# A layer norm centred by one matmul, its weights and biases folded away, and projections in 64-row tiles

## The reference, cut to what matters

```
def layernorm(x, w, b):                      # over the 64 channels of a position
    mu = mean(x); var = mean(square(x - mu))
    return (x - mu) * rsqrt(var + EPS) * w + b
x_ln = layernorm(x, ln1_w, ln1_b)
q, k, v = split(einsum('bhwc,oc->bohw', x_ln, qkv_w))          # 4 heads of 16
attn = softmax(q k / sqrt(16)); out = attn v                   # full attention, 1024 x 1024 per head
x = x + proj_w out + proj_b
x_ln2 = layernorm(x, ln2_w, ln2_b)
x = x + fc2_w gelu(fc1_w x_ln2 + fc1_b) + fc2_b                # fc1: 64 -> 128
t = t + window_attention(norm(t)) + bu       # 8 heads, 32 keys a query; norm without weights
t = t + recurrence(norm(t))                  # W x, batch norm, 1024 steps of sigmoid(wx + V y)
```

## Time and profile before

| | before |
|---|---|
| runs | 498.24, 501.23, 499.96: median 499.96 us |
| profiled execution | 499.44 us, its span 497.6 us |
| TensorE busy | 445.2 us (89%), granted clock 0.977 on the mean |
| VectorE busy | 327.3 us (66%), of that 166.6 in the 256 row maxima |
| ScalarE busy | 289.9 us (58%) |
| GpSimd busy | 12.9 us, all at the start |
| chain that ended last | 63% TensorE, 24% VectorE, 7% ScalarE, 3% DMA |

### The profile page before, as it was taken

The page is one execution under the profiler, slowest core; times in us unless marked ns, Lnnn a source line. Parts: engine busy times, 40 slices in busy tenths (PEclk is TensorE's granted clock), DMA queues, the critical chain, the costliest instruction groups (busy, mean ns, idle before and its releaser), DMA issues.

```text
span 497.6 us, 7934 instructions
## 1 busy us (share of the span) xinstructions
PE 445.2 (89%) x3257; PEld 176.3 (35%) x3257; DVE 327.3 (66%) x605; ACT 289.9 (58%) x499; POOL 12.9 (3%) x15
## 2 busy tenths in 40 slices
PE   7786999979999998899999996999999889986883
PEld 2323322223234332232243432232433323542583
DVE  2599887999778566598688474798522654524414
ACT  4342677747774673566955771678586656083342
POOL 9000000000000000000000000000000000000000
PEclk9898999999999999899999998999999999999997
DMA  7200180004500000017100000000000000000003
GB/s 293 57 1 2 29 162 3 0 2 100 91 2 1 1 1 1 1 29 147 16 2 1 1 1 2 1 1 0 3 1 1 1 0 2 1 1 1 1 1 86
DMA packets 6196, 13.09 MB, mean 26 GB/s; under 512 B 1296, under 2 KB 3600, under 8 KB 6032
## 3 DMA queue, kind: packets, MB, share of 16 engines
q1 hardware_dynamic: 6160, 12.58, 11.3%
HBM read 9.07 MB, written 3.41 MB: 25 GB/s over the span
## 4 chain that ended last, share of the span: by engine, by line
PE 63%; DVE 24%; ACT 7%; DMA 3%; issue 2%; SPq 1%; DVEq 0%; ACTq 0%
DVE part_max L1181 10%; PE O L750 9%; PE R L798 6%; PE T L735 5%; PE T L715 4%; PE R L907 3%; PE R L654 3%; PE R L735 3%; PE R L646 3%; PE R L868 2%; PE R L715 2%; PE R L882 2%; PE T L626 2%; PE R L895 2%; DMA KX<-qk_scratch 2%
## 5 line engine op out<-in xcount | busy, mean ns | idle before, releaser
L1181 DVE TENSOR_REDUCE part_max<-T 128x1 f32<-128x512 f32 x166 | 107.0, 681 | 25.3 <-PE T L715 25.2
L1041 ACT ACTIVATE probs<-T 128x512 f32<-128x512 f32 x149 | 83.8, 600 | 26.8 <-PE T L735 26.4
L1041 ACT ACTIVATE probs<-R 128x512 f32<-128x512 f32 x107 | 60.7, 601 | 31.2 <-PE R L735 31.0
L750 PE MATMUL O<-probs,VT 128*32 128x512 f32 x512 | 68.3, 606 | 0.0
L1181 DVE TENSOR_REDUCE part_max<-R 128x1 f32<-128x512 f32 x90 | 59.6, 682 | 3.9 <-PE R L715 3.9
L715 PE MATMUL T<-KX,QX 96*128 96x512 bf16 x166 | 56.2, 387 | 4.1 <-DVE part_max L1181 2.1
L735 PE MATMUL T<-QX,KX 99*128 99x512 bf16 x149 | 51.4, 386 | 3.9 <-DVE part_max L1181 1.8
L735 PE MATMUL R<-QX,KX 99*128 99x512 bf16 x107 | 37.2, 382 | 0.5 <-ACT VT L1026 0.3
L715 PE MATMUL R<-KX,QX 96*128 96x512 bf16 x90 | 31.3, 384 | 0.6 <-DVE part_max L1181 0.3
L715 PEld LDWEIGHTS T<-KX,QX 96*128 96x128 bf16 x166 | 15.1, 98 | 43.2 <-DVE part_max L1181 15.7
L798 PE MATMUL R<-xp,abd 128*128 128x512 f32 x64 | 30.0, 600 | 0.2 <-DVE xp L1150 0.2
(11 more groups left out here) (220 smaller groups left out, 636.1 us busy)
## 6 DMA issues: line engine op xcount, KB each, us to landing
qk_scratch<-qk_part SPq DMA_DIRECT2D x6, 384.0 KB, 4.5
zs<-early SPq DMA_DIRECT2D x1, 2048.0 KB, 9.2
QX<-qk_scratch SPq DMA_DIRECT2D x3, 384.0 KB, 5.3
KX<-qk_scratch SPq DMA_DIRECT2D x3, 384.0 KB, 7.0
result<-probs SPq DMA_DIRECT2D x2, 512.0 KB, 5.1
s_rest<-rest SPq DMA_DIRECT2D x1, 882.0 KB, 13.1
X<-x SPq DMA_DIRECT2D x2, 384.0 KB, 13.0
QX<-qk_scratch SPq DMA_DIRECT2D x3, 256.0 KB, 7.8
```

The source lines that it names most:

```text
L750: last = mm(O[h * HP:(h + 1) * HP, :], VT[b % 2][:, j, h, :], probs[:, u % 2, h, :], start=(j == 0), stop=(j == KT - 1))
L1041: A(probs[:, u % 2, h, :], ring["scores", b, u, h], ACT.Exp, scale=HD ** -0.5).then_inc(g["exp_done"], 1)
L1181: nc.vector.tensor_reduce(part_max[:, row, kh:kh + 1], ring["max_piece", b, half, i], AX_X, ALU.max).then_inc(g["max_red"], 1)
```

## The change

A norm has one VectorE instruction where it had two or three. `center`, the unit matrix less `mean_c`, takes the place of `mean_c` in the first product, so PSUM holds the centred rows at once; ScalarE squares them from PSUM, and VectorE makes the normalised rows from PSUM and the reciprocal root. The norm's weight goes into that instruction as its scalar. The norm's bias goes behind the products: `wq`, `wk` and `wfc1` are multiplied by the bias once, and the result is the bias of the ScalarE copy (`qk_bias`), of the Gelu (`fc1_bias`), and, for V, through the output projection, of `proj_bias`. These need four one-column products in the first projection and three in `products`.

Q, K and fc1 are made in 64-row tiles. PSUM bank R0 now holds the positions of half 0, Q in its lower 64 partitions and K in its upper 64, and bank R1 those of half 1, the other way round. So the three parts are written to DRAM by four transfers an image instead of two, and, as `RUNS` pairs the parts anew, read back by eight instead of six. The places of all four tables are new.

```
-RUNS = (((0, 2), (1, 1), (2, 0)), ((0, 1), (1, 0)), ((0, 0),))
+RUNS = (((0, 0), (1, 1)), ((0, 1), (0, 2)), ((1, 0), (2, 0)))
-FIRST = {"mean_c": P, "vectors": len(VECTORS), "eye": C, "wq": P, "wk": P, "wv": P}
+FIRST = {"mean_c": P, "center": P, "vectors": len(VECTORS), "eye": C, "wq": P, "wk": P, "wv": P}
 MAX_AT = (                          # one line of each table is shown
-        118, 118, 118, 119, 119, 119, 121, 121, 121, 123, 126, 127, 127, 132, 134, 134, 135, 135, 135, 139, 139, 139,
+        112, 112, 116, 117, 117, 117, 118, 118, 118, 119, 122, 122, 125, 127, 129, 130, 132, 137, 137, 137, 137, 139,
 LAYER_AT = (
-    0, 0, 3, 5, 15, 16, 21, 320, 316, 318, 328, 334, 343, 346, 348, 353, 353, 371, 384, 402, 411, 413, 421, 424,
+    0, 1, 1, 4, 9, 14, 14, 320, 320, 321, 323, 326, 337, 342, 350, 352, 353, 370, 370, 406, 408, 411, 411, 413,
...
+        def qk_rows(q, half):
+            return half_rows(q ^ half)
...
             def relayout(b):
                 for half in range(2):
-                    sp.dma_start(scratch[b, half].rearrange("q r d h n -> (d h) (q r) n"),
-                                 qk_rows[half_rows(half), :, :]).then_inc(g["qk_dram"], 16)
+                    for q in range(2):
+                        sp.dma_start(scratch[b, half, q].rearrange("r d h n -> (d h) r n"),
+                                     qk_part[qk_rows(q, half), half, :, :]).then_inc(g["qk_dram"], 16)
...
                     for q, dst in enumerate((QX[b % 2], KX[b % 2])):
+                        parts = sorted({term[q] for term in run_})
+                        p0, n = parts[0], len(parts)
+                        for again in range(len(run_) // n):
+                            at = row + again * HD
+                            sp.dma_start(dst[at:at + n * HD, :, :, :].rearrange("p a h n -> p a (h n)"), ...
...
             def ln_mean(b, which, i):        # TensorE
-                mm(ln_bank(b, which, i, 0), t["mean_c"], ln_in(b, which, i), start=True, stop=True).then_inc(g["ln_mean"], 1)
+                mm(ln_bank(b, which, i, 0), t["center"], ln_in(b, which, i), start=True, stop=True).then_inc(g["ln_ctr"], 1)
             def project(b):                  # TensorE
+                    for half in range(2):    # first image only
+                        for q, w in enumerate(("wq", "wk")):
+                            last = mm(bias_bank(half)[qk_rows(q, half), 0:1], t[w][half_rows(half), half_rows(half)], v["ln1_b"][half_rows(half), :],
+                                      start=True, stop=True)
+                        last.then_inc(g["bias_mm"], 1)
-                mm(R[:, 0, :], t["wq"], x_ln[:], start=True, stop=True).then_inc(g["qk_mm"], 1)
-                mm(R[:, 1, :], t["wk"], x_ln[:], start=True, stop=True).then_inc(g["qk_mm"], 1)
+                for half in range(2):
+                    for q, w in enumerate(("wq", "wk")):
+                        last = mm(R[qk_rows(q, half), half, :], t[w][half_rows(half), half_rows(half)], x_ln[half_rows(half), :],
+                                  start=True, stop=True)
+                    last.then_inc(g["qk_mm"], 1)
             def fc1(b):                      # TensorE
-                    last = mm(pair(b)[:, half, :], t["wfc1"][:, half, :], x_ln[:], start=True, stop=True)
+                    last = mm(pair(b)[:, half, :], t["wfc1"][half_rows(half), half, :], x_ln[half_rows(half), :], start=True, stop=True)
             def products():                  # TensorE
+                mm(R[:, 1, 0:1], t["wv"], v["ln1_b"], start=True, stop=True)
+                mm(R[:, 1, 1:2], t["wfc1"][0:C, 0, :], v["ln2_b"][0:C, :], start=True, stop=True).then_inc(g["fold_mm"], 1)
...
+                pe.wait_ge(g["fold_done"], 2)
+                mm(R[:, 1, 2:3], t["wproj_c"], v_bias[:], start=True, stop=True).then_inc(g["fold_mm"], 1)
             def ln_square(b, which, i):      # ScalarE
-                A(ln_bufs(b, which, i)["ln_q"], ln_bufs(b, which, i)["ln_d"], ACT.Square).then_inc(g["ln_sq"], 1)
+                A(ln_bufs(b, which, i)["ln_q"], ln_bank(b, which, i, 0), ACT.Square).then_inc(g["ln_sq"], 1)
             def project(b):                  # ScalarE
-                    A(hi_rows[:, q, :], R[:, q, :], ACT.Copy).then_inc(g["qk_hi"], 1)
+                    A(hi_rows[:, half, :], R[:, half, :], ACT.Identity, bias=qk_bias[:, half:half + 1]).then_inc(g["qk_hi"], 1)
-            def ln_mean(b, which, i):        # VectorE
-                TT(ln_bufs(b, which, i)["ln_d"], ln_in(b, which, i), ln_bank(b, which, i, 0), ALU.subtract).then_inc(g["ln_ctr"], 1)
             def ln_scale(b, which, i):       # VectorE
-                TT(ln_dst(b, which, i), buf["ln_d"], buf["ln_r"], ALU.mult).then_inc(g["ln_norm"], 1)
                 if which < 3:
-                    dve.wait_ge(g["ln_norm"], ln_no(b, which, i) + 1)
-                    TS(x_ln[:], ln_dst(b, which), v[f"ln{which}_w"], v[f"ln{which}_b"], ALU.mult, ALU.add).then_inc(g["ln_out"], 1)
+                    last = STT(dst, centered, v[f"ln{which}_w"], buf["ln_r"], ALU.mult, ALU.mult)
+                else:
+                    last = TT(dst, centered, buf["ln_r"], ALU.mult)
+                last.then_inc(g["ln_norm"], 1)
             def project(b):                  # VectorE
-                    TT(qk_rest[:, q, :], R[:, q, :], hi_rows[:, q, :], ALU.subtract).then_inc(g["qk_rst"], 1)
+                    STT(qk_rest[:, half, :], R[:, half, :], qk_bias[:, half:half + 1], hi_rows[:, half, :], ALU.add, ALU.subtract).then_inc(g["qk_rst"], 1)
...
+    arr["center"] = np.eye(P, dtype=f) - arr["mean_c"]
```

More of the change, by code:

```diff
@@ L435, in ln_dst @@
         def ln_dst(b, which, i=0):
+            if which < 3:
+                return x_ln[:, :]
             if which == 3:
                 return xn
-            return ln_bufs(b, which, i)["ln_d"] if which < 3 or (b, which) == (B - 2, 4) else xh[:, ln_cols(b, which, i)]
+            return ln_bufs(b, which, i)["ln_d"] if (b, which) == (B - 2, 4) else xh[:, ln_cols(b, which, i)]
         def pair(b):
@@ L447, in build @@
         LAID = 4 * H0 - 1
+        QK_READS = sum(len(r) // len({term[q] for term in r}) for r in RUNS for q in range(2))
         def laid(h, n):
@@ L692, in relay @@
                         for half in range(2):
-                            rows = sel[half_rows(half), q, r, :, h:C:H0].rearrange("p t d -> p (t d)")
-                            last = mm(lay_bank(q, half)[0:KQ, :], rows, qk_rows[half_rows(half), PARTS * q + r, :],
+                            rows = sel[qk_rows(q, half), q, k, :, h:C:H0].rearrange("p t d -> p (t d)")
+                            last = mm(lay_bank(q, half)[0:KQ, :], rows, qk_part[qk_rows(q, half), half, k, :],
                                       start=(k == 0), stop=(k == PARTS - 1))
@@ L1013, in project @@
                 elif b:
[L1014 to L1017 removed]
+                    act.wait_ge(g["qk_dram"], 64 * (b - 1))
+                else:
+                    act.wait_ge(g["bias_done"], 2)
+                for half in range(2):
+                    act.wait_ge(g["qk_mm"], 2 * b + half + 1)
+                    A(hi_rows[:, half, :], R[:, half, :], ACT.Identity, bias=qk_bias[:, half:half + 1]).then_inc(g["qk_hi"], 1)
             def project_v(b):
@@ L1320, in _ @@
             dve.wait_ge(g["first_in"], 16)
-            run({"masks": masks, "relay": relay, "ln_mean": ln_mean, "ln_scale": ln_scale, "project": project, "split": split,
+            run({"masks": masks, "relay": relay, "ln_scale": ln_scale, "project": project, "split": split,
                  "o_norm": o_norm_, "round": round_keys, "wx": wx_part, "max_piece": max_piece, "max_neg": max_neg,
@@ L1448 @@
     arr["wproj"] = wp
+    arr["wproj_c"] = both(g["L0_conv_proj_w"].T)
     w1 = np.zeros((P, 2, P), f)
```

109 lines of the change are left out of this document (59 added, 50 removed), and 18 rows, old and new, of the table LAYER_AT.

## The result

The changed kernel took 484.38 us (median of 4 runs, 480.5 to 488.32) against 500.6 of before: the ratio is 0.9645, 95% interval 0.9579 to 0.9711. Run twice more beside the experiments it stood at 0.9718 (0.9647 to 0.9789) and 0.9701 (0.9651 to 0.975). The forecast was 489.5, a ratio of 0.978: the sign was right, the gain was too small. The ratios and intervals leave out executions over 1.5% above the fastest of their kernel, here the one of 488.32 us, which is also the profiled one (span 486.5, TensorE's mean granted clock 0.973), so the end in its trace is worse than in most.

The account below looks back on a forecast made before the run. VectorE bounds 25 to 125 us, TensorE 125 to 390, chains through the engines both ends; -3.1 + 0.9 - 0.75 - 1.0 - 4.2 - 2.2 = -10.35 from 499.44 gives 489.1, plus 0.5 for the median, rounded: 489.5 us; range 483.5 to 495.5.

Parts of the forecast that it names:

- Part 1: First norm and projection, 0 to 22 us: one merged normalising instruction and tiled projection bring the low parts earlier, -3.1 us.
- rival E: First norm: the memset holds the normalising instruction, 2.4 us less gain, 491.9 us; counted within the forecast's 0.58.
- B: Tiles don't overlap as the nearest rows do: 0.85 us back at six places, 494.6 us; 0.19 shared by three rivals.
- Part 2: At 37 us: three products for the folded biases stand unhidden on TensorE around the weight products, +0.9 us.
- Part 3: Second image's norm, projection and transfers, 44 to 77 us: 1.03 + 0.6 gained, 0.9 given back to writes, -0.75 us.
- rival D: Transfers cost by their number: +5.2 - 0.9 us at 77 us, 493.8 us; 0.19 shared by three rivals.
- Part 4: Third image, 77 to 125 us: the same removal on VectorE, transfers stay hidden, -1.0 us.
- Part 5: TensorE's stretch, 125 to 390 us: -3.4 for fc1 and projection tiles, 0.8 of idle time back, -4.2 us.
- Rival A: 125 to 390 us: lighter VectorE shrinks TensorE's idle by 4 to 8 us, 482 to 486 us; chance 0.13.
- Rival C: ScalarE's exponentials or the new order hold TensorE, 125 to 390 us gains nothing, 493.7 us; 0.19 shared by three rivals.
- Rival G: New places stop TensorE's in-order queue between 125 and 390 us: slower, 503 at 10% idle, 509 at 12%; chance 0.06.
- Part 6: The end, 390 to 470 us: fc1 tiles -0.9, third norm -0.7, fourth norm -0.6, together -2.2 us.

Follow-up runs that it names:

- e7: Changed kernel plus an idle VectorE subtraction, result never used, at the 17 places where the real one stood: 0.9691 of before, 484.78 us.
- e8: Kernel before with GpSimd's memset of KX put behind the first image's x_ln: 502.44 us, one execution.

## Why the forecast was off

Part 1 (-3.1): right, -3.29. The normalising instruction took 0.75 beside the memset, so rival E fell, and the projection's 8 records took 1.09 at a clock of 1.00, so B fell. What the prediction did not see is that the clock fell behind it, at 20 us, and took back 1.3 in the profiled execution.

Part 2 (+0.9): right, +0.89 for the length of these products; between the row maxima on either side of them it is 0.7. Three products stood alone on TensorE.

Part 3 (-0.75): -1.9 was measured (from -1.28 at the first image's first transposed maxima, 43.30 in before, to -3.22 at the second image's first row maximum), and the term that failed is the +0.9 for the writes. Answering to the earlier trace rows, the four writes and the row maxima that wait for the reads:

```profile
55.71 2.63 SPq L570 DMA_DIRECT2D qk_scratch<-qk_part  x4
...
60.81 0.34 SPq L582 DMA_DIRECT2D QX<-qk_scratch  x1
...
72.99 0.60 PE L737 MATMUL R<-KX,QX 96*128 96x512 bf16 x2
```

```profile
73.41 1.29 DVE L1216 TENSOR_REDUCE part_max<-R 128x1 f32<-128x512 f32 x2 [2.96 <-PE R L737]
```

The same two of before, the first read and the first product that needs the reads:

```profile
64.51 0.34 SPq L568 DMA_DIRECT2D QX<-qk_scratch  x1
...
76.20 0.61 PE L715 MATMUL T<-KX,QX 96*128 96x512 bf16 x2 [0.30 <-DMA KX<-qk_scratch]
```

The first read was issued 5.10 us after the first write, where with two writes of twice the size it was 5.45: nothing given back. The eight reads took 0.5 more than the six (12.18 and 11.69 us from the first one's issue to the first product that needs them), so writes and reads together cost 0.14, not 0.9. The split itself came 2.1 earlier, where 1.6 was forecast. VectorE was dry for 2.96 us (3.33 before), so rival D fell. That the sum of the first three parts is right within 0.3 (-3.22 against -2.95) is luck: this error and the clock's 1.3 cancel.

Part 4 (-1.0): right, -1.14 to the end of the projection back.

Part 5 (-4.2): the step that failed; 10.5 was measured. Both of its terms were wrong. "-3.4" for the tiles: fc1's share of it, 2.6, was worth 0.3, as ScalarE's queue decides fc2; the projection's share was not measured. "I let 0.8 come back" took VectorE's and the norms' relief as something that could at most shrink 14.3 us of idle time; the runs show that a norm between TensorE's products holds TensorE wherever too little work stands between its two products, and that in the new places 10.4 us hung on the nine subtractions: 6.4 of idle time and 4.0 of busy time, mostly at the low clock that followed the first wait. So the premise that "the latency of a norm counts in full only at both ends" failed. The prediction priced a shorter norm against the idle time of the old order, 14.3 us, of which only 1.9 stood ahead of variances, and not against what the new order would idle without it. By busy and idle time the gain even looks as forecast for the tiles (TensorE 6.43 less busy: 3.4 of tiles, some 2.7 of clock), which is bookkeeping, not cause: take fc1's tiles away and only 0.3 goes. Nor did the "some 247 us of work" of the prediction's signs follow from its own sum, 246.78 less 3.4 for the tiles; 240.35 was measured.

Rival A had the size (idle down by 4 to 8 us, 482 to 486 in all) and the wrong cause: VectorE's load, which by e7 costs nothing in the middle. Rival C described correctly what happens to fc1, and missed the rest. Rival G, the new places as a loss, is true of the places alone: 1% slower with the old arithmetic. The prediction took the places for neutral, because most had moved by less than five of 320 (38 of the 241 places of `MAX_AT` differ by five to eleven); they were what turned a shorter norm into time.

Part 6 (-2.2): right while the clock was up, -2.24. The clock at 412 and 443 us took back up to 5.5 in the profiled execution.

What stays open: why the clock falls in one execution and not in another at the same place, though the order of work and the gap are the same; how much of the 4.0 us of busy time an execution with the subtraction but without that spell of the low clock would keep; and which of the new places carries most; the tables were exchanged as a whole.

## What to carry to other kernels

On an in-order engine, price a removed instruction by what the engine behind it has to do meanwhile: with enough work between the two ends of the chain it is worth nothing, with too little it is worth its duration, its place in the other engine's queue and perhaps the clock. A schedule made for one latency hides the gain of a shorter one, so arithmetic and order have to be timed together, and a 2 x 2 of the two tells more than either alone. To tell load from latency, put the same instruction back where nobody waits for it.

## What the hardware showed

- TensorE's granted clock fell to 0.50 behind idle gaps of 1.44 us (at 202 us in before) and 1.62 us (at 301), with work on both sides of them; 32 records then took 5.36 instead of 3.66 us. The same gaps left the clock at 1.00 in other executions (e8; 1.63 us at 189 in the changed kernel), and so did 2.75 us at 434. With clock-keeping products in the two gaps of before, the trace has no spell there and ten runs were 0.6% faster.
- Where the clock stays up, the middle of the program repeats to 0.02 us between executions: 250.56, 250.56 and 250.54 in the three traces of the changed kernel, whose spans are 486.5, 488.0 and 484.1. They differ in the spells of low clock at both ends; over all 14 executions the time follows the mean granted clock.
- Two casts of 128x512 beside a GpSimd memset of 3 partitions took 4.34 us instead of 0.75; a memset that touches 3 partitions holds an instruction on 128.
